# Transposing MoE gates in 32x32 squares on VectorE, padding a 24-row product to 128 rows, and joining TensorE's inserts

## What is computed

```python
A_norm = relu((A + A.T) * 0.5); D = sum(A_norm, axis=1)
L_norm = eye(N) - D^-0.5 * A_norm * D^-0.5
x = x + relu(L_norm @ (layernorm(x) @ W))          # x: (8, 2048, 128)
z = layernorm(x)
probs = softmax(z @ router_w.T); the two largest, scaled to a sum of 1 -> combine[token, e]
y = z
for e in range(8):
    y = y + combine[:, e:e+1] * (gelu(z @ w1[e] + b1[e]) @ w2[e] + b2[e])
out = x + y
```

## Time and profile before

| | |
|---|---|
| median of 3 runs | 954.29 us (953.29 to 954.32) |
| the profiled execution | 954.83 us, span 953.1 us |
| instructions | 15352 |
| TensorE busy | 895.1 us |
| VectorE busy | 645.7 us |
| ScalarE busy | 517.2 us |
| GpSimd busy | 311.8 us |
| mean granted TensorE clock | 0.986 of 2.4 GHz |

### The profile page before, as it was taken

The page is one execution under the profiler, slowest core; times in us unless marked ns, Lnnn a source line. Parts: engine busy times, 40 slices in busy tenths (PEclk is TensorE's granted clock), DMA queues, the critical chain, the costliest instruction groups (busy, mean ns, idle before and its releaser), DMA issues.

```text
span 953.1 us, 15352 instructions
## 1 busy us (share of the span) xinstructions
PE 895.1 (94%) x4446; PEld 723.6 (76%) x4446; DVE 645.7 (68%) x1558; ACT 517.2 (54%) x899; POOL 311.8 (33%) x312
## 2 busy tenths in 40 slices
PE   4766799999999999999999979999999999999996
PEld 3765588888887888878888757777777777777774
DVE  3986644756877733242424388888888888888886
ACT  3665232344444321222111378888888888888885
POOL 0699235555575634374443320000000000000000
PEclk9996899999999999999999999999999999999999
DMA  9983255686584346866776765777777777777771
GB/s 285 321 255 125 100 203 206 254 279 204 188 281 163 100 164 250 274 243 250 259 265 252 283 210 185 263 263 264 264 263 263 262 265 267 268 268 269 268 268 44
DMA packets 93022, 222.98 MB, mean 234 GB/s; under 512 B 8856, under 2 KB 59568, under 8 KB 81072
## 3 DMA queue, kind: packets, MB, share of 16 engines
q1 hardware_dynamic: 86752, 211.59, 63.1%
q0 software_dynamic: 2560, 8.39, 2.2%
q10 hardware_dynamic: 3664, 2.43, 0.9%
HBM read 157.89 MB, written 64.49 MB: 233 GB/s over the span
## 4 chain that ended last, share of the span: by engine, by line
PE 81%; DVE 7%; POOL 4%; issue 4%; ACT 2%; DMA 1%; DVEq 0%; ACTq 0%; POOLq 0%
PE bank L913 11%; PE bank L915 11%; PE bank L914 11%; PE bank L1290 7%; PE bank L1277 6%; PE bank L1292 6%; PE bank L1291 6%; PE bank L1279 6%; PE bank L1278 6%; POOL col_sum L543 3%; PE bank L858 2%; PE bank L330 2%; DVE y_lo L699 2%; PE bank L1298 1%; PE bank L1287 1%
## 5 line engine op out<-in xcount | busy, mean ns | idle before, releaser
L1366 DVE TENSOR_TENSOR gated<-c_all,act_h 128x512 f32<-128x512 f32 x256 | 177.4, 693 | 50.5 <-ACT act_h L1328 47.4
L1328 ACT ACTIVATE act_h<-bank,b_sb 128x512 f32<-128x512 f32 x256 | 176.4, 690 | 63.0 <-PE bank L1279 56.2
L1371 DVE TENSOR_TENSOR g_lo<-gated,g_hi 128x512 fp32r<-128x512 f32 x256 | 175.1, 684 | 0.2
L1335 ACT ACTIVATE g_hi<-gated 128x512 fp32r<-128x512 f32 x256 | 159.2, 622 | 4.3 <-DVE gated L1366 4.3
L1262 POOL DMA_DIRECT2D out<-fin x32 | 24.3, 761 | 372.4 <-DVE fin L1379 367.3
L913 PE MATMUL bank<-y_hi,stage 128*128 128x512 f32 x256 | 111.7, 436 | 3.1 <-DVE y_lo L699 3.1
L1290 PE MATMUL bank<-g_hi,w_hi 128*128 128x512 f32 x256 | 107.4, 420 | 5.5 <-DVE g_lo L1371 5.4
L1002 POOL TENSOR_TENSOR rstd<-var_eps,neg_half 128x4 f32<-128x4 f32 x32 | 48.9, 1527 | 180.0 <-DVE var_eps L1039 179.3
L1277 PE MATMUL bank<-z_e,w_hi 128*128 128x512 f32 x256 | 103.8, 405 | 1.2 <-ACT act_h L1328 1.2
L913 PE MATMUL bank<-y,stage 128*128 128x512 f32 x256 | 104.5, 408 | 0.0
L1007 POOL TENSOR_SCALAR z<-x,mv,rstd 128x128 f32<-128x128 f32 x128 | 102.7, 817 | 3.4
(11 more groups left out here) (118 smaller groups left out, 1582.2 us busy)
## 6 DMA issues: line engine op xcount, KB each, us to landing
c_all<-c_scratch SPq DMA_DIRECT2D x64, 1024.0 KB, 8.2
s_scratch<-stage SPq DMA_DIRECT2D x14, 2048.0 KB, 8.4
stage<-s_scratch SPq DMA_DIRECT2D x14, 2048.0 KB, 8.1
z_e<-z_scratch SPq DMA_DIRECT2D x32, 512.0 KB, 7.0
z_scratch<-z_hl SPq DMA_DIRECT2D x31, 512.0 KB, 2.7
x_raw<-in_x SPq DMA_DIRECT2D x32, 256.0 KB, 7.7
x_res<-in_x SPq DMA_DIRECT2D x32, 256.0 KB, 7.2
r_e<-res_scratch SPq DMA_DIRECT2D x32, 256.0 KB, 2.7
```

The source lines that it names most:

```text
L1328: act.activation(v.act_h[e % R][:, :], ps_h[e % 2][:, :], ACT.Gelu, bias=v.b1_sb[:, e:e + 1]).then_inc(gelu_done, 1)
L1335: act.activation(v.g_hi[e % R][:, :], v.gated[e % R][:, :], ACT.Copy).then_inc(hi_done, 1)
L1366: dve.tensor_tensor(out=v.gated[e % R][:, :], in0=v.c_all[s][:, e, :], in1=v.act_h[e % R][:, :], op=ALU.mult).then_inc(gated_done, 1)
L1371: dve.tensor_tensor(out=v.g_lo[e % R][:, :], in0=v.gated[e % R][:, :], in1=v.g_hi[e % R][:, :].bitcast(FP32), op=ALU.subtract).then_inc(lo ...
```

## The change

VectorE transposes the gates of a batch of four units in one instruction, square by square: `gate_parts` is widened from 24 to 32 columns for each of the 16 groups of 128 tokens (the eight new ones are zeroed once by GpSimd), so that its 128 x 512 elements are 4 x 16 squares of 32 x 32. `gate_x` then holds, in partition 32g + e, the gates of the tokens 32g to 32g + 31 of each group. Four DMAs for each batch, one for each g, store 24 partitions of it in pieces of 32 elements. So that this is one pattern for four units, `c_dram` is laid out (3E, unit, 512), and the logits of the first half's units are put in reversed slots. SP issues the stores in units 7, 11, ..., 31, ScalarE those of the last batch behind expert 13 of the expert stage. `turn_gate`, `copy_gate` and `gates_in` go.

`b2_parts` and both `c_parts` have 128 rows. GpSimd zeroes them in unit 20; only the first 24 rows are ever loaded.

In `between`, what stood behind steps 1 to 5 (first turn of x, two groups) stands together behind step 2; the second turn of x goes from step 5 to step 6, behind the first project; the third and fourth group go from steps 10 and 13 to step 12, behind `turn_z`.

```diff
-    v.c_dram = nc.dram_tensor("c_scratch", (U, 3 * E, CW), FP32, kind="Internal").ap()
+    v.c_dram = nc.dram_tensor("c_scratch", (3 * E, U, CW), FP32, kind="Internal").ap()
...
-        v.gate_parts = sb("gate_parts", [P, T, 3 * E], FP32, at)
+        v.gate_parts = sb("gate_parts", [P, T, 32], FP32, at)
...
-        v.gate_t = [sb(f"gate_t{i}", [3 * E, CW], FP32, at) for i in range(2)]
+        v.gate_x = sb("gate_x", [P, T, 32], FP32, at)
...
-        v.b2_parts = sb("b2_parts", [3 * E, P], FP32R, at)
+        v.b2_parts = sb("b2_parts", [P, P], FP32R, at)
...
-        v.c_parts = [sb(f"c_parts{i}", [3 * E, CW], FP32R, at) for i in range(2)]
+        v.c_parts = [sb(f"c_parts{i}", [P, CW], FP32R, at) for i in range(2)]
...
+    def slot(u):
+        return 3 - u % 4 if u < MB else u % 4
+
+    def store_gates(eng, batch):
+        eng.wait_ge(gate_turned, batch + 1)
+        w = min(unit(4 * batch), unit(4 * batch + 3))
+        rows = v.c_dram[:, w:w + 4, :].rearrange("e w (q g t) -> g e (w q) t", q=Q, g=4)
+        for g in range(4):
+            eng.dma_start(rows[g], v.gate_x[32 * g:32 * g + 3 * E, :, :]).then_inc(gate_out[half(4 * batch)], 16)
...
+            if u >= 7 and u % 4 == 3:
+                store_gates(sp, (u - 7) // 4)
             if u == U - 2:
                 v.load_first(sp)
             if u:
                 store_unit(u - 1)
...
-        S_AT = (2, 4, 10, 13)
...
-            wait(pe, gate_copied, gates_before[u + 2] if u + 2 <= U else U - 4)
...
-            if ks and i in (1, 5):
-                wait(pe, gate_copied, gates_before[u])
-                pr.turn_x(pe, ks[i // 4])
-            if ks and i in (6, 9):
-                pr.project(pe, ks[i // 9])
-            if ahead and i in S_AT and S_AT.index(i) < st.n_groups(u + 1):
-                st.turn_group(pe, u + 1, S_AT.index(i))
-            if i in (8, 11) and gates_in(u):
+            groups = range(st.n_groups(u + 1)) if u + 1 < MB else range(0)
+            if i == 2:
                 if ks:
-                    pe.wait_ge(pr.xt_copied, ks[1] + 1)
-                turn_gate(gates_in(u)[i // 11], u - 1)
-            if u and i == 12:
-                turn_z(u - 1)
+                    pr.turn_x(pe, ks[0])
+                for g in groups[0:2]:
+                    st.turn_group(pe, u + 1, g)
+            if ks and i == 6:
+                pr.project(pe, ks[0])
+                pr.turn_x(pe, ks[1])
+            if ks and i == 9:
+                pr.project(pe, ks[1])
+            if i == 12:
+                if u:
+                    turn_z(u - 1)
+                for g in groups[2:4]:
+                    st.turn_group(pe, u + 1, g)
             if u and i == 15:
                 route(u - 1)
...
-        v.tail_tensor = {0: [(turn_early, U - 6)], 1: [(turn_early, U - 5)], 5: [(turn_z, U - 1)], 7: [(route, U - 1)],
-                         12: [(turn_late, U - 4)], 13: [(turn_late, U - 3)], 14: [(turn_late, U - 2)],
-                         15: [(turn_late, U - 1)]}
+        v.tail_tensor = {5: [(turn_z, U - 1)], 7: [(route, U - 1)]}
...
+        v.tail_scalar = {6: [(copy_z, U - 1)], 8: [(store_last, U - 1)], 9: [(exps, 7)], 13: [(store_last_gates, 7)]}
...
+        pool.wait_ge(v.summed, v.all_groups)
+        pool.memset(v.gate_parts[:, :, 3 * E:], 0.0).then_inc(pad_made, 1)
...
+            if u == MB + 4:
+                pool.wait_ge(acc_done, MB)
+                v.zero_rows(pool)
...
-            wait(dve, gate_turned, 4 * batch)
+            wait(dve, gate_turned, batch)
...
             dve.tensor_tensor(out=low.bitcast(FP32R), in0=gate, in1=high, op=ALU.subtract).then_inc(gate_done, 1)
+            dve.wait_ge(gate_done, batch + 1)
+            dve.wait_ge(pad_made, 1)
+            if batch > 4:
+                dve.wait_ge(gate_out[1], 64 * (batch - 4))
+            else:
+                wait(dve, gate_out[0], 64 * batch)
+            dve.transpose(v.gate_x[:, :, :].rearrange("p t c -> p (t c)"),
+                          v.gate_parts[:, :, :].rearrange("p t c -> p (t c)")).then_inc(gate_turned, 1)
...
+    def zero_rows(pool):
+        for rows in (v.b2_parts, v.c_parts[0], v.c_parts[1]):
+            pool.memset(rows[:, :].bitcast(FP32), 0.0).then_inc(zero_made, 1)
...
-        unit_gates = v.c_dram[bass.ds(u, 1)]
+        unit_gates = v.c_dram[:, bass.ds(u, 1), :]
...
-                         unit_gates[:, first:first + E // 2, :].rearrange(
-                             "a e n -> (a e) n").partition_broadcast(P)).then_inc(c_all_in[2 * s + half], 16)
+                         unit_gates[first:first + E // 2, :, :].rearrange(
+                             "e a n -> e (a n)").partition_broadcast(P)).then_inc(c_all_in[2 * s + half], 16)
```

More of the change, by code:

```diff
@@ L736, in graph_stage @@
     acc = [v.banks[0], v.banks[1]]
-    ps_c, ps_z, ps_r = [v.banks[4], v.banks[7]], v.banks[6], v.banks[7]
+    ps_z, ps_r = v.banks[6], v.banks[7]
     acc_done = st.acc_done
@@ L1159, in expert_stage @@
     b2_placed = sem("b2_placed")
+    zero_made = sem("zero_made")
     w_hi_made = sem("w_hi_made")
```

51 lines of the change are left out of this document (10 added, 41 removed).

## The result

The changed kernel takes 995.29 us (median of 4 runs, 988.68 to 1000.23), the kernel before in the same comparison 953.79 (952.96 to 954.32): a ratio of 1.0432, 95% interval 1.0404 to 1.046. The forecast was 924.0, in a range of 918 to 932. The change makes the kernel 4.3% slower. The profiled execution took 994.36 us, its span is 992.7.

The account below looks back on a forecast made before the run. TensorE was taken to bound the kernel, busy 895.1 of 953.1 us. Savings of 11.8 + 12.3 + 3.0 + 2.0 + 1.2 = 30.3 us, taken from the median 954.29, gave 924.0, range 918 to 932.

Parts of the forecast that it names:

- the bound on the price of the pieces: Gates' broadcast loads: 2 KB pieces could cost at most 1.18 times as much, with the engines' share under 0.9.
- the rival on the loads: Expert units: broadcast in four 2 KB pieces makes loads the bound, slower, 1011 us at a factor of 2; chance 0.04.
- its turning point: Expert units: from a factor of about 1.6 on the broadcast loads, a unit would be longer than before.
- The pointer in the last sentence of the forecast: Expert stage: if the time is over 932, look first at L1290's waits for g_lo.
- The gates' transposes: Graph stage: 26 TensorE inserts of 0.455 us each go, 11.8 us saved.
- VectorE's transposes: Graph stage: eight replacing transposes of 128x512, 0.7 us each (bounds 0.35 and 2.8), hidden.
- The stores: Gates' stores, 28 of 32 on SP: 1 us per issue fits in SP's waits for res, costing nothing.
- The product with b2: Expert units: 128 rows instead of 24 remove 0.41 us in each of 30, 12.3 us saved (0 to 13.1).
- The start of the expert stage: Six gate inserts and their waits go there, partly offset by VectorE and ScalarE: 3.0 us saved (1 to 5).
- Joining, unit 0 and the turns of x: Inserts standing together save 0, unit 0's shorter wait 2.0 us, waits for x in units 8 to 15 1.2.
- That the product with b2 stays as dear (936.3): Rival, expert units: the 0.41 us comes from waits or opening a sum, so 12.3 us stay; chance 0.08.

Follow-up runs that it names:

- e3: The kernel before with each scratch row 64 bytes longer, so the broadcast reads four 2 KB pieces 2112 bytes apart: 955.58 us, ratio 0.9998.
- e2: The changed kernel with one unused row for each (gate, expert), so the gates' rows lie 66 KB apart, not 64: 928.64 us, ratio 0.9721.
- e14: The changed kernel with 68 KB from row to row of the gates' scratch: 932.50 us, ratio 0.9764.
- e5: The kernel before with the changed kernel's order of TensorE's inserts, the gates still turned by TensorE: 951.39 us, ratio 0.9966.
- e7: e2 with the product with b2 over 24 rows again: 940.1 us, ratio 0.9842.
- e10: e9 with VectorE's transposes of a batch moved behind the diagonal block, z_low and the logits of their unit: 926.22 us, ratio 0.9699.
- e1: The changed kernel with the old order of scratch rows (8 KB in one piece), gates stored by 16 small DMAs for each batch: 954.01 us, ratio 0.9988.
- e17: The changed kernel with the scratch ordered batch outermost, five unit places in a row of which four are used, 10 KB row to row: 927.06 us.
- e9: e2 with the last batch's four gate stores issued by GpSimd behind its last unit, not by ScalarE: 926.82 us, ratio 0.9708.
- e4: The kernel before with only b2_parts and c_parts widened to 128 rows, zero from row 24 on: 943.12 us, ratio 0.988.

## Why the prediction was wrong

**The step that failed** is the bound on the price of the pieces, in the rival on the loads: "the pieces could cost 1.18 times as much". It was worked out from the first 100 us, where small pieces run at 301 GB/s for a full share, and it took the price for one of piece size. Size was the wrong quantity (e3). Where the pieces lie was the right one, and no row of the kernel before has four pieces 64 KB apart, so the bound did not cover it. The measured factor is 1.42 for all bytes. Put on c_all alone, two of a unit's three MB, it is 1 + 0.42 / 0.67 = 1.63, an estimate. The landing times say the same or more: 14.8 / 8.2 = 1.8. The rival had named the resource and the place (waits at L1277 for z_e, c_all over 12 us), and gave it a chance of 0.04.

**A second step of that rival failed too:** its turning point, "from a factor of about 1.6", counts the engines' share alone, as if a load costs nothing until the engines are full. By that count a factor of 1.42 on all bytes makes 8.7 x 1.42 = 12.4 us of a unit, 0.7 over the 11.70 that e2 reached; the unit took 13.99, with a share of 0.87. The rest is the landing time. In e2, where z_e lands after 7.2 us, it has this much room between issue and use:

```profile
673.18 0.34 SPq L1220 DMA_DIRECT2D z_e<-z_scratch  x1
...
682.24 0.39 PE L1270 MATMUL bank<-z_e,w_hi 128*128 128x512 f32 x1
```

That is 9.06 us. A median landing of 12.2 us does not fit into it. e14 stands near the turning point: z_e lands after 8.3 us, the full share is worth 268 / 0.80 = 335 GB/s over its stretch, so a byte costs only 1.09 times as much as before, and TensorE already waits:

```profile
PE bank L1270 <- DMA z_e<-z_scratch: 4.0, 5, 1.1
```

Its units took 11.90 us. So with an unknown access pattern the bound had to be the factor at which the kernel breaks, and that is read from a load's landing time and its room, not from the engines' share. The pointer in the last sentence of the forecast, to L1290's waits for g_lo, led nowhere: they are 5.3 us in all, 5.4 before.

**Point by point,** by the traces of the kernel before and of e2, where the loads are out of the way. The spans are 953.1 and 927.3, 25.8 apart; the forecast was 30.3.

- *The gates' transposes, 11.8 us forecast:* 10.0 (e5 to e7). The price of an insert was right, since a unit with two of them became 0.91 us shorter in the units 7, 8, 12, 15 and 16 and in all later ones that have them. It failed in unit 11, which did not give the 0.91 but grew by 0.82, and in unit 14, which has no gate insert and grew by 0.53. "TensorE hardly waits" was true with the inserts in place; without them waits appear or grow in these two units.
- *VectorE's transposes, 0.7 us forecast, hidden:* 0.711 each and hidden in the graph stage, as far as e10 tells, which moved them and gained nothing clear. The size was taken from the wrong row: the earlier trace rows are two operations in 1.29 us, the 0.69 stands in the earlier trace rows.
- *The stores, nothing:* nothing. "1 us each" was right as a median (1.0) and not as a bound (up to 3.9). e1 shows what the same kind of issue costs without cover.
- *The product with b2, 12.3 us forecast:* 13.06 in the 29 units between the third and the last product, 0.45 each. The reading of one product, 0.41, was 0.04 low.
- *The start of the expert stage, 3.0 us forecast:* -0.6 in e2, 1.1 in e17, 2.0 in e9. The two waits for the gates and act_h did go. But a wait of 2.19 us for GpSimd's z is new, and behind it and behind the wait for g_lo (3.03 us; 2.83 before, 3.03 in e4) the clock falls to 1.2 GHz for a time. Over the stretch it is 0.91 to 0.96, where it was 1.00 before. TensorE's timeline in e2, and windows behind the two waits:

```profile
541.16 0.66 PE L852 MATMUL bank<-ident,z 128*128 128x128 f32 x4 [2.19 <-POOL z L978]
...
555.11 0.50 PE L1283 MATMUL bank<-g_hi,w_hi 128*128 128x512 f32 x1 [3.03 <-DVE g_lo L1364]
```

```profile
542.60:545.80 3.20, 3.20 (x9) 2.45 (x8) 2.04 (x4) 3.04 (x6) 0.00 (x0) 0.50 0.00 0
...
556.20:559.40 3.20, 3.20 (x11) 2.61 (x10) 2.78 (x11) 1.30 (x3) 0.00 (x0) 0.50 0.03 8
```

  The term counted what goes and took no account of the clock; its lower bound of 1 was too high. An estimate from e2 and e17, where 0.05 of the clock was worth 1.64 us: at 1.00 the stretch would take about 37 us, some 2.4 less than before, so most of what is missing from the 3.0 went to the clock.
- *Joining, unit 0 and the turns of x, 0 + 2.0 + 1.2 = 3.2 us forecast:* 3.4 (e5), of which 2.07 in unit 0 and 0.87 in the units 8 to 15. The wait at L427 is 3.7 us, as forecast. One sentence rested on rows that are not the ones it names: the earlier trace rows are seven waits of 8.2 us over the whole span, and the "three times, 2.8 us in all, 1.9 the longest" are those of the graph stage in it. The term came out right to 0.3.
- *That the product with b2 stays as dear (936.3):* refuted by e4. The sentence of the Trainium skill that spoke for it (TensorE: Matmul & The Clock Gate, Why this matters for your kernels) does not hold for a single product over 24 rows among products over 128: it costs 0.45 us more than one over 128. The rule of the other page (TensorEngine Tiling (Array Packing), Key Properties), that a change of mode drains the engine, fits: the late starts lay on both sides of the product and went with the row count. The runs show the price and not the draining itself.

The sum over e2: the graph stage ends 13.0 us earlier (15.0 forecast for transposes, joining, unit 0 and turns together), the start of the expert stage is 0.6 longer (3.0 shorter forecast), the units are 13.1 shorter (12.3 forecast), and 0.3 is left at the end. That makes 25.8. The changed kernel has 65.4 us more in its span than e2: 66.2 more from the third product with b2 to the last, 1.0 less at the start of the expert stage, and 0.2 at the end. Of the 66.2, TensorE's waits for loads are 45.5; the granted clock of 0.96 over 405.62 us is worth about 16, an estimate.

## What to carry to other kernels

Before rows are put apart in DRAM, look at where the pieces that one transfer reads together lie modulo 8 KB; here a multiple of 8 KB made the load take 1.7 to 1.8 times as long, slowed the transfers beside it, and one unused row of 2 KB for each (gate, expert) put it right. For a load with two buffers, compare the time to its landing with the time between its issue and its use; the share of busy DMA engines does not show how near the limit is. A store that becomes simpler by a new layout is paid for by its readers: here the gates are written once and read by all 128 partitions. When an insert is taken away from the bounding engine, the waits that it covered come out; price it by e5's kind of run, unit by unit, and not by its duration times its count.

## What was not expected of the hardware

- The place of 2 KB pieces modulo 8 KB: 14.4 to 15.0 us for a broadcast of 1 MB from four pieces at one place, 9.4 at two, 7.7 to 9.0 at four. Over the stretch from the third product with b2 to the last, the bytes for a full share of the engines were worth 238 to 267 GB/s at one place, 335 at two and 345 to 359 at four.
- z_e and r_e, contiguous and untouched, slowed with it (7.0 to 12.2 us, 2.7 to 6.0). They share its queue and its engines; which of the two passes the delay on was not tried.
- A product over 24 rows among products over 128 costs 0.45 us more than one over 128 rows.
- The issue of a store of 384 pieces of 128 bytes took 0.4 to 3.9 us on SP in the graph stage (1.54 in unit 11, 6.17 for four), 0.86 on ScalarE for the 96 pieces of e1's stores (13.83 for 16), 0.76 on GpSimd (3.03 for four of 384) and 0.48 on ScalarE at the start of the expert stage (1.91 for four). So the time of an issue is not set by its pieces alone; what else sets it was not tried.
